# Rows of x prepared and multiplied one at a time in the streamed stage, and four weights' squares in other places

## The reference

```python
def ada_gcn(xn, weight, bias):                 # xn: x as (512 nodes, 64, 128)
    x_norm = xn / maximum(norm(xn, axis=-1), 1e-12)
    mean_sim = einsum('nbl,mbl->nm', x_norm, x_norm) / B
    # for each node keep the k = 153 most similar other nodes
    A = where(mask, mean_sim, 0); deg = A.sum(axis=0); dinv = rsqrt(deg)
    An = dinv[:, None] * A * dinv[None, :]
    return einsum('sd,sbl->dbl', An, einsum('nbl,lo->nbo', xn, weight)) + bias
x = layernorm(x + ada_gcn(x, adj, bias))
# second layer: attention-like graph kernels of h = x
z_l, z_g, v = h @ W_lang.T, h @ W_grav.T, h @ W_V.T
K = w_l * rowstochastic(relu(cosine(z_l))) + (1 - w_l) * rowstochastic(exp(-dist2(z_g)))
x = layernorm(x + (K @ v) @ W_O.T)
```

## Time and profile before

| | |
|---|---|
| median of 3 runs | 974.02 us (973.75 to 976.36) |
| the profiled execution | 975.82 us, span 974.1 us |
| busy, share of the span | PE 95%, DVE 76%, ACT 54%, POOL 32% |
| mean granted clock of TensorE | 0.988 |
| streamed stage, rows 0 and 1 | to about 110 us |
| rows 2 and 3, both picks, weights | about 110 to 200 us |

### The profile page before, as it was taken

One profiled execution on the slowest core, in us unless ns is written; L12 is line 12 of the kernel. 1 busy time (PEld: TensorE's weight loads), 2 busy tenths in 40 slices (PEclk: granted clock), 3 DMA queues, 4 the chain that ended last, 5 costly groups with the idle time before them and its releaser, 6 DMA issues.

```text
span 974.1 us, 18755 instructions
## 1 busy us (share of the span) xinstructions
PE 927.9 (95%) x6858; PEld 543.4 (56%) x6858; DVE 735.7 (76%) x1650; ACT 525.0 (54%) x911; POOL 311.9 (32%) x396
## 2 busy tenths in 40 slices
PE   3999999899999999999999999999999999999994
PEld 3777786455555555555555546464646464646451
DVE  5787497557787878787877777777777877786866
ACT  6787746575454555555545454545454545453531
POOL 3677372235140404040405050505050505050410
PEclk9999999899999999999999999999999999999997
DMA  6464120010313131222131313131222222121211
GB/s 261 176 212 156 62 88 14 31 44 2 87 52 80 53 78 59 72 63 80 49 92 37 106 27 104 31 98 38 92 43 86 47 82 58 71 43 43 43 44 43
DMA packets 85857, 71.80 MB, mean 74 GB/s; under 512 B 64704, under 2 KB 64832, under 8 KB 83776
## 3 DMA queue, kind: packets, MB, share of 16 engines
q1 hardware_dynamic: 85824, 71.38, 24.5%
HBM read 38.86 MB, written 16.78 MB: 57 GB/s over the span
## 4 chain that ended last, share of the span: by engine, by line
issue 51%; PE 17%; POOL 13%; DVE 12%; ACT 5%; POOLq 1%; DMA 1%; DVEq 0%; ACTq 0%
POOL arena L435 6%; PE bank L527 2%; PE bank L264 2%; POOL arena L440 2%; PE bank L534 2%; PE bank L533 2%; PE bank L265 2%; PE bank L266 2%; ACT arena L1122 2%; POOL arena L474 1%; POOL part_rest L455 1%; DVE stats L1599 1%; ACT arena L1127 1%; PE bank L497 1%; POOL rn_parts L457 1%
## 5 line engine op out<-in xcount | busy, mean ns | idle before, releaser
L264 PE MATMUL bank<-arena 128*128 128x512 f16 (+2 forms) x1056 | 292.9, 302 | 9.1 <-DVE arena L1770 5.9
L265 PE MATMUL bank<-arena 128*128 128x512 f16 (+2 forms) x1056 | 292.2, 301 | 0.0
L266 PE MATMUL bank<-arena 128*128 128x512 f16 (+2 forms) x1056 | 292.1, 301 | 0.0
L264 PE MATMUL pair<-arena 128*128 128x512 f16 (+1 forms) x400 | 152.0, 380 | 0.0
L265 PE MATMUL pair<-arena 128*128 128x512 f16 (+1 forms) x400 | 151.7, 380 | 0.0
L266 PE MATMUL pair<-arena 128*128 128x512 f16 (+1 forms) x400 | 151.4, 379 | 0.0
L264 PEld LDWEIGHTS bank<-arena 128*128 128x128 f16 x1056 | 103.3, 98 | 74.2 <-DVE arena L1770 7.7
L266 PEld LDWEIGHTS bank<-arena 128*128 128x128 f16 x1056 | 103.6, 98 | 63.7 <-issue 1.4
L457 POOL TENSOR_TENSOR sq_parts<-cf,zero 128x4 bf16<-128x4 f32 x16 | 3.3, 208 | 421.7 <-DVE cf L1700 421.7
L265 PEld LDWEIGHTS bank<-arena 128*128 128x128 f16 x1056 | 103.5, 98 | 53.5 <-issue 0.8
L1133 ACT ACTIVATE arena<-bank 128x512 f16<-128x512 f32 x64 | 38.1, 596 | 141.5 <-PE bank L266 141.5
(11 more groups left out here) (336 smaller groups left out, 1917.3 us busy)
## 6 DMA issues: line engine op xcount, KB each, us to landing
arena<-in_x SPq DMA_DIRECT2D x33, 1024.0 KB, 5.5
out_dram<-arena SPq DMA_DIRECT2D x15, 1024.0 KB, 4.3
arena<-in_w_grav_t SPq DMA_DIRECT2D x1, 1024.0 KB, 7.3
arena<-in_w_lang_t SPq DMA_DIRECT2D x1, 1024.0 KB, 5.3
arena<-in_w_v SPq DMA_DIRECT2D x1, 1024.0 KB, 8.0
arena<-in_w_o_t SPq DMA_DIRECT2D x1, 1024.0 KB, 7.6
out_dram<-arena SPq DMA_DIRECT2D x4, 256.0 KB, 2.4
arena<-arena SPq DMA_TRANSPOSE x60, 3.2
```

What stands on the lines that cost most here:

```text
L264: pe.matmul(dst, ah, bh, start=start, stop=False)
L265: pe.matmul(dst, ah, bl, start=False, stop=False)
L266: return pe.matmul(dst, al, bh, start=False, stop=stop)
```

## The change

In the streamed stage `normalise`, `high`, the low part and `gram` go by rows (VectorE by rows for chunks 0 and 1, then by two rows), each with its own wait. Spreads and item sums stand one chunk nearer to their use (spread c + 1 and item sums c + 2 within chunk c, squares c + 2). The first chunk is loaded in two halves. TensorE gets 16 matmuls on constants at the start. Of the squares, weights 1 and 0 stay before `cross_out`, weight 2 and the adjacency go behind the copies to S, weight 3 goes to VectorE (multiply and reduce); the maximum and the scales move behind the first and the second count of `pick`, and TensorE's part of it behind chunks 2 and 4. The diff, cut to its core:

```diff
+squares2 = at(144 * KIB, [KB, NODES])
+squares3 = at(184 * KIB, [KB * NODES])
...
-    for c in range(SLOTS):
+    for half in range(2):
+        mine = slice(half * CL // 2, (half + 1) * CL // 2)
+        sp.dma_start(xc[0][:, mine, :], x_chunk[0][:, mine, :]).then_inc(s["first_half"] if half == 0 else x_loaded[0], 16)
+    for c in range(1, SLOTS):
...
-        sp.wait_ge(s["xn_l_ready"], c - SLOTS + 1)
+        sp.wait_ge(s["xn_l_ready"], (c - SLOTS + 1) * CL)
...
-    sp.wait_ge(s["xn_l_ready"], NC - 3)
+    sp.wait_ge(s["xn_l_ready"], (NC - 3) * CL)
     sp.dma_start(w_raw[2], wv.rearrange("(k p) e -> p k e", p=P)).then_inc(s["w_in2"], 16)
-    sp.wait_ge(s["xn_l_ready"], NC - 2)
+    sp.wait_ge(s["xn_l_ready"], (NC - 2) * CL)
     sp.dma_start(w_raw[3], woT.rearrange("(k p) e -> p k e", p=P)).then_inc(s["w_in3"], 16)
...
-    pool.wait_ge(s["xn_h_ready"], 1)
-    for t in range(CL):
-        low = pool.tensor_tensor(xn_l[:, t, :], xc[0][:, t, :], xn_h[:, t, :], ALU.subtract)
-        low.then_inc(s["first_low"] if t < CL - 1 else s["xn_l_ready"], 1)
-    for c in range(1, NC):
-        pool.wait_ge(s["xn_h_ready"], c + 1)
-        o = slice(c * CL, (c + 1) * CL)
-        pool.tensor_tensor(xn_l[:, o, :], xc[c % SLOTS], xn_h[:, o, :],
-                           ALU.subtract).then_inc(s["xn_l_ready"], 1)
+    for c in range(NC):
+        for t in range(CL):
+            pool.wait_ge(s["xn_h_ready"], c * CL + t + 1)
+            pool.tensor_tensor(xn_l[:, c * CL + t, :], xc[c % SLOTS][:, t, :], xn_h[:, c * CL + t, :],
+                               ALU.subtract).then_inc(s["xn_l_ready"], 1)
...
+    pe.wait_ge(s["consts_made"], 1)
+    for i in range(16):
+        pe.matmul(bank[4][:, 0:P], ones[:], ident[:], start=True, stop=True)
...
     pe.wait_ge(s["picks_made"], 4)
...
     def spread(c, slot):
...
         pe.wait_ge(s["rinv_ready"], c + 1)
-        wait(pe, s["xn_ready"], c - 1)
+        wait(pe, s["xn_ready"], c * CL - CL)
...
-    def rows_01(c, slot, first=False, last=False):
-        if not isinstance(c, int) or c + 2 < NC:
-            spread(c + 2, slot)
-        if first:
-            for t in range(CL // 2):
-                pe.wait_ge(s["first_low"], t + 1)
-                gram(c, (0, 1), first=True, ts=range(t, t + 1))
-        else:
-            pe.wait_ge(s["xn_l_ready"], c + 1)
-            gram(c, (0, 1), ts=range(0, CL // 2))
-        if not isinstance(c, int) or c + 3 < NC:
-            item_sums(c + 3, 1 - slot)
-        if first:
-            pe.wait_ge(s["xn_l_ready"], 1)
-        gram(c, (0, 1), last=last, ts=range(CL // 2, CL))
+    def rows_01(c, slot, t, first=False, last=False):
+        pe.wait_ge(s["xn_l_ready"], c * CL + (t + 1))
+        gram(c, (0, 1), first=first, last=last, ts=range(t, t + 1))
...
+    rows_01(0, 0, 0, first=True)
+    rows_01(0, 0, 1)
...
-    rows_01(0, 0, first=True)
+    rows_01(0, 0, 2)
+    rows_01(0, 0, 3)
+    rows_01(1, 1, 0)
+    spread(2, 0)
+    rows_01(1, 1, 1)
+    item_sums(3, 1)
+    rows_01(1, 1, 2)
+    rows_01(1, 1, 3)
...
-        for t in (1, 2):
-            rows_01(j * 2 + t, t % 2)
-    for c in range(NC - 3, NC):
-        rows_01(c, c % 2, last=(c == NC - 1))
+        for u in (2, 3):
+            c = j * 2 + u
+            rows_01(c, u % 2, 0)
+            spread(c + 1, (u + 1) % 2)
+            rows_01(c, u % 2, 1)
+            item_sums(c + 2, u % 2)
+            rows_01(c, u % 2, 2)
+            rows_01(c, u % 2, 3)
+    for c in range(NC - 2, NC):
+        for t in range(CL):
+            rows_01(c, c % 2, t, last=(c == NC - 1))
+            if t == 0 and c + 1 < NC:
+                spread(c + 1, (c + 1) % 2)
     finish_diagonal(0)
...
-    pe.wait_ge(s["magn_ready"], 5)
-    pe.wait_ge(s["magn_x"], 1)
-    pe.transpose(bank[4][0:8, 0:P], magn[:], ident[:]).then_inc(s["magn_all_ready"], 1)
     for c in range(NC):
         gram(c, range(2, KB), first=(c == 0), last=(c == NC - 1))
-        if c == 1:
+        if c == 2:
+            pe.wait_ge(s["magn_ready"], 4)
+            pe.wait_ge(s["magn_x"], 2)
+            pe.transpose(bank[4][0:8, 0:P], magn[:], ident[:]).then_inc(s["magn_all_ready"], 1)
+        if c == 4:
...
             pe.wait_ge(s["magn_root"], 2)
...
-    def square(c):
-        act.wait_ge(x_loaded[c % SLOTS], 16 * (c // SLOTS + 1))
-        wait(act, s["ssum_ready"], c - 1)
-        act.activation(sq[c % 2], xc[c % SLOTS][:, 0:CL // 2, :], ACT.Square).then_inc(s["sq_ready"], 1)
-        wait(act, s["ssum_ready"], c)
-        act.activation(pair23[:], xc[c % SLOTS][:, CL // 2:, :], ACT.Square).then_inc(s["sq_ready"], 1)
+    def square(c, half):
+        if c == 0 and half == 0:
+            act.wait_ge(s["first_half"], 16)
+        else:
+            act.wait_ge(x_loaded[c % SLOTS], 16 * (c // SLOTS + 1))
+        if half == 0:
+            wait(act, s["ssum_ready"], c - 1)
+            act.activation(sq[c % 2], xc[c % SLOTS][:, 0:CL // 2, :], ACT.Square).then_inc(s["sq_ready"], 1)
+        else:
+            wait(act, s["ssum_ready"], c)
+            act.activation(pair23[:], xc[c % SLOTS][:, CL // 2:, :], ACT.Square).then_inc(s["sq_ready"], 1)
...
-    def high(c):
-        act.wait_ge(s["xn_ready"], c + 1)
-        act.activation(xn_h[:, c * CL:(c + 1) * CL, :], xc[c % SLOTS], ACT.Copy).then_inc(s["xn_h_ready"], 1)
-    square(0)
-    square(1)
+    def high(c, ts):
+        for t in ts:
+            act.wait_ge(s["xn_ready"], c * CL + t + 1)
+            act.activation(xn_h[:, c * CL + t, :], xc[c % SLOTS][:, t, :], ACT.Copy).then_inc(s["xn_h_ready"], 1)
+    square(0, 0)
+    square(0, 1)
+    square(1, 0)
+    square(1, 1)
...
-    square(2)
-    for c in range(NC):
+    square(2, 0)
+    high(0, range(0, CL // 2))
+    square(2, 1)
+    root(1)
+    for c in range(1, NC):
+        repeat(c)
+        high(c - 1, range(CL // 2, CL))
+        if c + 2 < NC:
+            square(c + 2, 0)
+            square(c + 2, 1)
+        high(c, range(0, CL // 2))
...
-            repeat(c + 1)
-        high(c)
-        if c + 3 < NC:
-            square(c + 3)
+    high(NC - 1, range(CL // 2, CL))
...
-    act.wait_ge(s["xn_l_ready"], NC - SLOTS + 1)
-    for n, i in enumerate((1, 0, 2, 3)):
+    act.wait_ge(s["xn_l_ready"], (NC - SLOTS + 1) * CL)
+    for i in (1, 0):
...
-        wait(act, s["magn_ready"], n)
+        wait(act, s["magn_ready"], 1 - i)
...
-    act.wait_ge(s["magn_ready"], 4)
-    act.activation(squares[:, 0, 0:P], adj_sb[:], ACT.Square,
-                   accum_out=magn[:, 4:5]).then_inc(s["magn_ready"], 1)
...
     cross_out(0)
     cross_out(1)
-    act.wait_ge(s["magn_ready"], 5)
-    act.wait_ge(s["xn_l_ready"], NC)
+    act.wait_ge(s["magn_ready"], 2)
+    act.wait_ge(s["xn_l_ready"], NC * CL)
...
         act.activation(dst, src, ACT.Copy).then_inc(s["S_ready"], 1)
-    act.wait_ge(s["scale_steps"], 2)
+    act.wait_ge(s["w_in2"], 16)
+    act.activation(squares2, w_raw[2], ACT.Square, accum_out=magn[:, 2:3]).then_inc(s["magn_ready"], 1)
+    act.wait_ge(s["magn_ready"], 3)
+    act.activation(squares2[:, 0, 0:P], adj_sb[:], ACT.Square,
+                   accum_out=magn[:, 4:5]).then_inc(s["magn_ready"], 1)
+    deviation(0)
+    act.wait_ge(s["scale_steps"], 3)
     act.activation(magn_top[:], magn_top[:], ACT.Sqrt).then_inc(s["magn_root"], 1)
...
     act.activation(magn_diag[:], ident[0:8, 0:8], ACT.Copy, scale=magn_top[:]).then_inc(s["magn_root"], 1)
-    deviation(0)
...
     def normalise(c):
...
-        dve.scalar_tensor_tensor(xc[c % SLOTS], xc[c % SLOTS], X_HAT,
-                                 bank[5 + c % 2][:].unsqueeze(1).broadcast_to([P, CL, NODES]),
-                                 ALU.mult, ALU.mult).then_inc(s["xn_ready"], 1)
+        n = 1 if c < 2 else CL // 2
+        for t in range(0, CL, n):
+            dve.scalar_tensor_tensor(xc[c % SLOTS][:, t:t + n, :], xc[c % SLOTS][:, t:t + n, :], X_HAT,
+                                     bank[5 + c % 2][:].unsqueeze(1).broadcast_to([P, n, NODES]),
+                                     ALU.mult, ALU.mult).then_inc(s["xn_ready"], n)
...
     dve.wait_ge(s["nrm_in"], NC)
...
-    dve.wait_ge(s["xn_l_ready"], NC)
+    dve.wait_ge(s["w_in3"], 16)
+    dve.wait_ge(s["xn_l_ready"], (NC - SLOTS + 2) * CL)
+    w_o = w_raw[3].rearrange("p k n -> p (k n)")
+    dve.tensor_tensor(squares3, w_o, w_o, ALU.mult).then_inc(s["scale_steps"], 1)
+    dve.wait_ge(s["scale_steps"], 1)
+    dve.tensor_reduce(magn[:, 3:4], squares3, AX.X, ALU.add).then_inc(s["magn_x"], 1)
+    dve.wait_ge(s["xn_l_ready"], NC * CL)
+    dve.wait_ge(s["magn_x"], 2)
     dve.memset(work[:, :, NODES:], PAD).then_inc(s["work_ready"], 1)
...
-    def pick(pair, n, between=lambda: None):
+    def pick(pair, n, between=lambda step: None):
...
-        between()
         for i in range(COUNTS):
...
+            between(i)
...
     fill_work(1, 3)
-    dve.wait_ge(s["magn_all_ready"], 1)
```

(18 more changed lines are left out.)

## The result

The changed kernel took 978.95 us in the median of 14 runs (976.45 to 984.23), the kernel before 973.96 beside it (970.52 to 977.37): ratio 1.0051, 95% interval 1.0035 to 1.0068, so 5.0 us slower and above the range of 970.0 to 977.0. The profiled execution after took 977.99 (span 976.2), that of before 975.82 (span 974.1): the pair shows 2.1 of the 5.0. A second profile of each came out as the first (978.1 and 975.9). Two later runs of the kernel before, 1384 and 1619 us at a mean granted clock of 0.66 and 0.56, were in a slow state of the core and are in no median or ratio.

The account below looks back on a forecast made before the run. TensorE was taken to bound the streamed loop. The stage would gain about 1.8 us, late scale factors would leave 0.5 of it, so the 974.02 median would become 973.5, range 970.0 to 977.0.

Parts of the forecast that it names:

- Where the gain goes: From first counts to all-reduce: late scale factors hold back most of the stage's 1.8 us, leaving 0.5 less.
- The low part comes by TensorE and ScalarE: Ahead of the all-reduce: GpSimd's last low part, 0.3 to 0.55 us sooner, decides over VectorE's need.
- The opening: Start of streamed stage: first low row at 19.2, first product at 20.35 instead of 23.84; stage gains about 1.8 us.
- Halves and warming at nothing: Opening: loading chunk 0 in halves and 16 warming matmuls were priced as worth nothing.
- The loop: Streamed chunks: all other engines stay under TensorE's 5.38 us a chunk, so row-by-row work costs nothing.
- Both rivals on ScalarE's rows: Streamed loop: rows at full duration, 975 us (chance 0.12); loop bound by ScalarE, 978 us (chance 0.13).
- Weight 3 on VectorE: Before the counts: two operations of 2.29 us, VectorE free at 110.1 to 111.2; nothing to 0.65 lost, taken as nothing.
- The scale factors: Inside the pick's first counts: ready at 119.7 against 117.8, so ScalarE starts on the weights 1.9 us later.
- The low blocks of weight 2: GpSimd's 16 low blocks, with SP's load and ScalarE's copy of x, carry on the 1.9 us lateness.
- TensorE's idle: Ahead of cross product 2: rows 2 and 3 done at 136.4, cross product at 138.0; TensorE keeps 0.3 of 1.8 us.
- Behind 168 us: Around the degrees: granted clock averages 0.66 over 168 to 183; main forecast left it so.
- the gain survived: Faster rival, chance 0.20: all-reduce follows VectorE (1.35 sooner), clock stays up at 168 and 179, giving 969 us.

Follow-up runs that it names:

- both repairs and the fillers: Changed kernel with scale factors one count sooner, GpSimd's mask behind chunk 1's low rows, unread matmuls in TensorE's four idle stretches: 967.95 us, ratio 0.9941.
- the first four experiments: Streaming part alone 1.0093, weights part alone 1.0047; changed kernel with factors one count sooner 1.0011, with idle ahead of cross product 2 filled 1.0022.
- the later experiments: Kernel before, stretches filled 0.9971; changed kernel: all filled 0.9987, GpSimd's mask moved 0.9998, no warming 1.0042, mask and factors moved 0.9952, these plus fillers 0.9941.

## Why the prediction was wrong

The chain was named rightly: late scale factors, GpSimd's low blocks, SP's load of x, ScalarE's copy, cross product 2, and so GpSimd's last low part ahead of the all-reduce. Three of its terms were too small, and a clock term was missing. The step that failed is the last of "Where the gain goes": "The low part comes by TensorE and ScalarE, 0.3 to 0.55 sooner, and it decides." It decided, but 3.3 later (158.15 against 154.88). Of that, 1.4 is cross product 2 (139.68 against 138.27, forecast 0.3 sooner), 0.9 lies between it and the last four low blocks, where the matmuls at half clock are, and 1.0 is in those blocks (3.52 against 2.56), which now run beside VectorE's selection at 155.23.

- **The opening, right.** First low row at 19.97 (19.2 predicted) and first product at 21.18 (20.35): the small loads landed 0.8 later. The stage gained 1.3 against 1.8 (the prediction's own terms, 109.73 less 108.05, give 1.7), inside its bounds. Halves and warming at nothing: shown for the warming, not tried for the halves. Weighed was the rule of the Trainium skill, "TensorE: Matmul & The Clock Gate", section "What's actually happening", that the throttled clock is the default and activity releases it. The trace agrees: with the sixteen matmuls done at 9.0, the eight item-sum matmuls at 9.64 took 1.03, against 1.84 without the warming. But the granted clock fell at 11.0, and the first products ran at half speed until 24.5, so this did not help the new order.
- **The loop, right.** 5.38 a chunk; two rows of ScalarE took 1.13 to 1.15. Both rivals on ScalarE's rows fall. (Their sums take 2.97 of other work a chunk, where the parts listed leave 4.83 − 1.80 = 3.03; nothing here hangs on it.) The Trainium skill, "VectorE: DVE Perf Modes", section "The TRN2 errata — SBUF-src ops pay a fixed extra latency per instruction", has a fixed cost between instructions; here four rows took 2.28 (at 101.85) where one instruction takes 1.89, and the chunk's slack covered it.
- **Weight 3 on VectorE, mis-sized.** "I take nothing"; its multiply took 3.08, not 2.29, and VectorE was free at 111.69, 1.1 later than the 110.6 at which ScalarE had written S. The multiply overlapped GpSimd's last low row (102.56 to 107.08 for the four), and the profile with both repairs and the fillers shows the same meeting from the other side.
- **The scale factors, mis-sized.** First weight predicted 1.9 late, measured 2.65 late; the distance from cross product 0 grew by 4.0. Of the 0.75 beyond, 0.5 is the smaller gain of the stage and the rest VectorE's late start.
- **The low blocks of weight 2, mis-sized.** I let three queues carry the 1.9 on unchanged. But the load of x left 3.6 late: from ScalarE's first weight to it lie 130.61 − 120.51 = 10.10 us, before 126.99 − 117.86 = 9.13. GpSimd's first eight blocks took 6.1 instead of 5.1: a block takes 0.66 alone and 1.15 while VectorE selects over two operands; before, most of that fell in the second eight blocks (VectorE's selection at 126.27, the load at 126.99), now all of it in the first (125.14). That this meeting costs the 1.0 is read from the traces; no run moved the blocks apart. Groups of GpSimd's lines in 126 to 127 after:

```profile
L408 POOL TENSOR_TENSOR arena<-arena 128x256 f16<-128x256 f32 x2 | 2.3, 1154 | 0.0
```

  The Trainium skill, "SBUF — State Buffer", section "Who interferes with whom", has a VectorE instruction with two SBUF inputs contend with a GpSimd instruction that reads SBUF, over a shared read interface; the trace agrees, with VectorE's pair of selections at 1.76 beside the blocks (1.28 at 154.82 before, where they run alone) and GpSimd's at 1154 ns.
- **TensorE's idle, the term that was left out.** Predicted were rows 2 and 3 done at 136.4 and cross product 2 at 138.0, so 1.6 us of idling, priced as a wait alone. Measured: 2.99 of idling, then 3 us at half clock and 3.23 for matmuls that take 1.96, 1.3 more. Filling it without touching the chain gave back 2.8 us of the median (1.0051 to 1.0022), some of it behind 168 us; sending the factors one count sooner, with 1.36 of idling left, gave 3.9. The fall is likely behind such an idle stretch and not certain: see the profile without the warming.
- **Behind 168 us.** I took the granted clock there as given unless the gain survived. The kernel before shows two groups in the 29 runs beside the first four experiments: 20 at a mean granted clock of 0.991 or more, 970.7 to 974.3 us, and 9 at 0.988 or less, 975.2 to 977.1. (Of the runs beside the later experiments, two lie between, at 0.990 and 973.7 and 974.1 us.) With its stretches filled, all are in the first group. The changed kernel's means can be compared with these only without the warming, since with it they contain the 0.007 of the opening: there it is at 0.986 to 0.989 in 11 of 12 runs, nearly always in the second group or just beside it. That is an inference from the means, since both profiles of before are of the second group: it would explain why a pair of profiles showed 2 us and the medians 5.

So of the 5.0 us, 1.6 stay when TensorE is kept busy in both kernels (0.9987 against 0.9971; the intervals overlap, so this size is rough). The other 3.4 or so went with the filling: the clock, and what its falls shift.

Open: why the clock's rise in the opening differs from run to run, why one idle stretch of 3.15 us cost no clock where four others of 2.90 to 3.15 did, and why the late chain makes the falls behind 168 nearly certain.

## What to carry to other kernels

Where a change moves a small result (a maximum, a scale factor) later to fit it between other work, follow it through every queue up to the engine that sets the end; here 2.65 us of lateness became 3.6 where two engines that disturb each other met at another place. Price an idle stretch of TensorE by its length and, as a chance, by what runs at half clock behind it, and try to fill it with matmuls nobody reads before rebuilding the order. Look at what stands ahead of the first work in each in-order queue: a wait for four small loads held 4 us here. One profile of each kernel can fall in different groups of their runs; compare mean granted clock and time over all runs, and make sure that the column starts to count at the same place in both kernels.

## What the runs showed of the hardware

A 1.00 in the column of the granted clock ahead of its first change says nothing: the first products before ran at half pace under it (0.31 for one of 128 columns), while the changed kernel shows 0.50 from 18 to 24 and, without its warming, 1.00 there at the same pace of the products. So two kernels' mean clocks can differ by 0.007 with no difference in pace. Sixteen early matmuls did bring the clock up (1.03 against 1.84 for eight matmuls at 9.64), but not for work that began 12 us later: it had fallen at 11.0. The rise came 3 us behind the first steady products in one profile and 9 us behind them in another. A stretch of about 3 us of idling was followed by half clock in four of five profiles. When VectorE's multiply and GpSimd's low row met, either could be the one to pay: 3.17 instead of 2.29 for the one, or 3.25 instead of 1.16 for the other. And filler matmuls cost the surrounding work nothing measurable where they fit in the idle time: with them the kernel before took 970.6 us instead of 973.7.
